# An audio tower on one core: head 4 looked up densely in every second batch, and two tables streamed through a ring

## The chip, the core and the metric

One core of a Trainium2 chip runs the whole program. The metric is the device time in microseconds of one execution.
## What is computed

For each of 32 batches: a tokenizer (four strided convolutions with a channel norm, an MLP that gives every time step a weight, and a pooling from 128 steps to 64 channels by the running sum of the weights), a recurrent mixer (a delta-rule attention over 128 rows of 64), and a feed-forward layer of eight heads with product keys. The last one is what the change touches:

```python
q = (x @ Wq_pk).reshape(b, n, P, HEADS, DIM_KEY).transpose(2, 0, 1, 3, 4)
sim = jnp.einsum('pbnhd,pkhd->pbnhk', q, pk_keys)              # 2 x 64 key scores of each row and head
scores, idx = jax.lax.top_k(sim, PK_TOPK)                      # the best 16 of either side
...
final_scores, pk_idx = jax.lax.top_k(score, FINAL_TOPK)        # the best 16 of the 256 sums
final_scores = jax.nn.softmax(final_scores, axis=-1)
...
k = jnp.einsum('bnhk,bnhkd->bnhd', kv_scores, keys_table[ind])   # 4096 rows of 64 for each head
v = jnp.einsum('bnhk,bnhkd->bnhd', kv_scores, values_table[ind])
```

k and v of a head then take part in a causal attention over the 128 rows. So each row needs, for each head, the weighted sum of 16 rows out of a table of 4096 rows of 128 numbers (key and value side by side).

## The kernel before

The weighted sum is made in two ways. Heads 0 to 4 (NG = 5) are **gathered**: DVE works out the 16 row numbers, POOL fetches 128 table rows with one indirect DMA (L1090), 16 of them a head and so 80 a batch, into one of three buffers `got`, and PE adds them up with 16 weighted matmuls (L1381; the trace shows 32 records) and a transpose (L1387). Heads 5 to 7 (`DENSE`, ND = 3) are **dense**: the whole table of the head lies in SBUF (`tab`, 16 KB in each partition for each head, loaded once), and a head goes through it in 16 units of 256 table rows. A unit is: PE makes the sums of both key scores and a rank distance for 256 x 128 pairs (`pair_scores`, L1337 and L1339, four bf16 matmuls into one of two banks), ACT takes the exponential (L1642), DVE sets those outside the chosen 16 to zero (L2203), and PE multiplies by the table (`table_sum`, L1359). ACT copies the head's sum out after its last unit (L1651). Before its units a dense head needs a distance of each key from the chosen ones (DVE, L2150 and L2155, twelve instructions a head), transposes (L1317, L1318), a split into three bf16 parts, and a trip of these parts through DRAM (`parts`) to the layout `stacked`, by 12 DMAs a head that SP issues.

All engines work on several batches at a time. Each stage of a batch (tokenizer, mixer, `route` for heads 0 to 3, `second` for heads 4 to 7, dense, sums of gathered heads, heads) is cut into hops. The tables `AT` (and `OWN` for the first three and last three batches) give each hop a position in a batch's time; batch b stands b * STEP later. `plan()` sorts all hops by position, and every engine's queue is written in that one order. A hop's position is no time on the chip: it only sets what stands before what in each queue. The order has the dense units of one batch follow on those of the batch before: the units run without a break over the whole program, with pieces of the other stages of other batches between them.

POOL holds nothing but the gathers. Before each head it waits for the row numbers (`s_rows`, `s_single`), and at each fourth gather for the buffer to be read (`s_summed`).

Of the kernel before, what the change touches and what calls it, by code (L numbers as in the profile page):

```python
# [20 lines left out]
ALU = mybir.AluOpType  # L21
ACT = mybir.ActivationFunctionType
# [17 lines left out]
DENSE = (5, 6, 7)  # L40
ND = len(DENSE)
NG = HEADS - ND
# [3 lines left out]
UNITS = ND * TILES  # L46
# [16 lines left out]
QUARTER = 4  # L63
PARTS = 4
# [74 lines left out]
def tower(nc, x, consts, pairs, w0, w1, w2, w3, cvec, mw1, mw2, mw3, mb1, mb2, mb3, stack, mix, bw, ba, bg, vec64,  # L139
          wo_attn, gn, wqpk, keys, wq, table, wo_ffn, parts, out):  # L140
    ctx = ExitStack()
    with ctx:
# [135 lines left out]
        tab = sb("tab", [P, ND, CHUNKS, P])  # L278
# [83 lines left out]
        s_stack = [sem(f"s_stack{i}") for i in range(2)]  # L362
        s_pairs = sem("s_pairs")
# [33 lines left out]
        block = ctx.enter_context(nc.Block())  # L397

# [31 lines left out]
        for n, k in enumerate(("xd", "proj", "lora", "ss", "tri", "p0", "t0", "p1", "t1", "p2", "t2", "p3", "t3", "p4", "t4",  # L430
# [8 lines left out]
        R2 = {k: n for n, k in enumerate(each_list + [  # L439
            "idx", "cand", "keys", "fin8", "codes", "code", "rep_f0", "rep_f1", "rep_f2", "rep_f3", "fin16_0", "fin16_1", "fin16_2", "fin16_3", "fidx",  # L440
            "place", "early", "shift", "pick_e0", "row_e0", "pick_l0", "row_l0",
            "row_d", "row_t", "rep_d", "row_h", "code0", "chosen", "code1", "depth", "code2", "code3"]
            + [f"{k}{i}{j}" for i in range(ND) for j in range(2) for k in ("miss", "near", "half", "dist")]
            + ["fsum", "frec", "weight", "w_t", "shifted"], 1)}
        NROUTE, NSECOND = len(R), len(R2)
# [20 lines left out]
        def group_hops(u):  # L466

            last = u == UNITS - 1
            return ([(f"v{u - 1}", 0.9)] if u else []) + ([(f"k{u - 1}", 0.4)] if u and u % TILES == 0 else []) + (
                [(f"p{u + 1}", 1.2)] if not last else []) + ([("s2", 0.1)] if u == TILES else []) + (  # L470
                [(f"x{u}", 0.6), (f"w{u}", 0.8)]) + ([(f"v{u}", 0.9), (f"k{u}", 0.4)] if last else [])
# [12 lines left out]
        def choose_hops(pieces):  # L484
            return ([("r0", 1.2), ("r1", 1.2), ("r2", 2.2), ("r3", 1.2), ("r4", 1.2), ("cands", 0.5), ("keys", 0.5), ("fin8", 0.8), ("codes", 1.2),
                     ("finx", 0.7), ("repf", 1.0), ("fin16", 0.8), ("fidx", 0.7), ("early", 0.5), ("shift", 0.4), ("e", 0.0)]
                    + [x for k in range(pieces) for x in ((f"e{k}", 1.0), (f"l{k}", 1.2), (f"lr{k}", 1.1))])
# [1795 lines left out]
```

## Time and profile before

| | us |
|---|---|
| median of 3 runs | 3446.4 (3445.68 to 3448.38) |
| span of the profiled execution | 3442.5 |
| PE busy / weight loads | 3091.9 (90%) / 2384.2 (69%) |
| DVE busy | 2856.3 (83%) |
| ACT busy | 2103.0 (61%) |
| POOL busy | 2469.3 (72%) |
| DMA engines, mean busy share | 0.27 at 71 GB/s |

Busy time of an engine is the time in which at least one of its instructions was running. An instruction's time holds its latency, and the next one may start before it ends, so a busy share near 90% is not yet a full engine. POOL's gap between two indirect DMAs is listed as "issue": it waits for nothing there. The profiled span lies 3.9 us under the median of the runs.

### The profile page before, as it was taken

The page shows a single profiled execution, that of the slowest core. Times are in us where ns is not written, and L with a number is a line of the kernel's source. Part 1 is how long each engine was busy: PE and PEld are TensorE (multiplying, and loading weights), DVE is VectorE, ACT ScalarE, POOL GpSimd, SP SyncE. Part 2 cuts the span into 40 slices and gives each one's busy share as a digit, 9 for nine tenths or more (in the row PEclk, how much of TensorE's full clock was granted, in tenths as well). Part 3 has the DMA queues.
Part 4 walks back from the last instruction along what each step waited for, and adds up shares of the span by engine and source line. Part 5 has one row for each costly group of instructions (what it writes and reads, how often), then busy time and mean ns, then how long its engine had stood idle before and what let it go on. Part 6 is the DMA issues. An engine that isn't in the chain of part 4 may idle for free.

```text
span 3442.5 us, 79362 instructions
## 1 busy us (share of the span) xinstructions
PE 3091.9 (90%) x25850; PEld 2384.2 (69%) x25850; DVE 2856.3 (83%) x14978; ACT 2103.0 (61%) x5921; POOL 2469.3 (72%) x2571
## 2 busy tenths in 40 slices
PE   9999999889999989999999999998999999888777
PEld 6776667677667666666767766776766676766666
DVE  3688888988888988888898888888888888888762
ACT  5456666666666666666566666666666666665333
POOL 0177777777777777777777777777777777777774
PEclk9999999999999999999999999999999999999888
DMA  7022222222222222222222222222222222222221
GB/s 159 11 74 71 72 66 69 74 74 76 69 74 61 74 75 75 74 69 69 65 75 73 75 68 75 61 74 74 74 75 69 71 64 75 75 75 68 66 77 41
DMA packets 307373, 245.84 MB, mean 71 GB/s; under 512 B 246600, under 2 KB 259440, under 8 KB 306832
## 3 DMA queue, kind: packets, MB, share of 16 engines
q0 software_dynamic: 81920, 167.94, 17.8%
q1 hardware_dynamic: 225040, 72.83, 9.1%
q8 instruction: 206, 3.38, 0.4%
q14 instruction: 207, 1.70, 0.2%
HBM read 230.06 MB, written 10.49 MB: 70 GB/s over the span
## 4 chain that ended last, share of the span: by engine, by line
POOL 53%; issue 19%; PE 16%; DVE 9%; ACT 4%; DMA 0%; POOLq 0%; SPq 0%; DVEq 0%; ACTq 0%
POOL got L1090 53%; PE bank L1359 3%; PE bank L1180 3%; DVE d_w L2203 1%; PE bank L1198 1%; PE bank L1109 1%; PE bank L1337 1%; PE bank L1339 1%; PE bank L1381 1%; DVE top L1938 1%; PE bank L1126 1%; DVE dist L2155 0%; DVE topi L1942 0%; DVE pick L2150 0%; ACT L1432 0%
## 5 line engine op out<-in xcount | busy, mean ns | idle before, releaser
L1090 POOL DMA_INDIRECT got<-in_table,rows x2560 | 2466.4, 963 | 936.9 <-issue 777.7
L1359 PE MATMUL bank<-d_w,tab 128*128 128x128 f32 x6144 | 1055.9, 295 | 136.5 <-DVE d_w L2203 128.9
L1359 PEld LDWEIGHTS bank<-d_w,tab 128*128 128x128 f32 x6144 | 827.4, 195 | 325.3 <-DVE d_w L2203 214.5
L2203 DVE SCALAR_TENSOR_TENSOR d_w<-bank,d_w 128x256 f32<-128x256 f32 x1536 | 633.6, 414 | 168.3 <-ACT d_w L1642 159.0
L1642 ACT ACTIVATE d_w<-bank 128x256 f32<-128x256 f32 x1536 | 579.6, 380 | 276.6 <-PE bank L1339 258.5
L1337 PE MATMUL bank<-stacked,stack_sel 128*128 128x128 bf16 x3072 | 428.5, 222 | 12.3 <-issue 11.5
L1339 PE MATMUL bank<-d_dist,sel 128*128 128x128 bf16 x3072 | 428.7, 222 | 0.0
L1180 PE MATMUL bank<-h,conv_w 128*128 128x512 f32 (+2 forms) x1024 | 330.6, 469 | 0.5 <-DVE h L1789 0.4
L1337 PEld LDWEIGHTS bank<-stacked,stack_sel 128*128 128x128 bf16 x3072 | 306.8, 100 | 35.0 <-issue 15.2
L2155 DVE TENSOR_REDUCE dist<-pick 128x32 f32<-128x512 f16 x384 | 261.7, 682 | 6.6
L1180 PEld LDWEIGHTS bank<-h,conv_w 128*128 128x128 f32 x1024 | 171.8, 189 | 119.7 <-issue 109.2
L1339 PEld LDWEIGHTS bank<-d_dist,sel 128*128 128x128 bf16 x3072 | 240.7, 99 | 0.0
L1381 PE MATMUL bank<-got,spread_w 128*32 128x128 f32 x5120 | 176.6, 277 | 52.6 <-DMA got<-in_table,rows 28.5
L1518 ACT ACTIVATE square<-bank,cbias 128x512 f32<-128x512 f32 (+2 forms) x96 | 48.7, 508 | 250.2 <-PE bank L1180 250.1
L1381 PEld LDWEIGHTS bank<-got,spread_w 128*32 128x32 f32 x5120 | 135.6, 110 | 90.9 <-issue 79.3
L2150 DVE TENSOR_TENSOR pick<-misses,key_codes 128x256 f16<-128x256 f16 x768 | 190.3, 282 | 0.0
L1432 ACT ACT_TABLE_LOAD x128 | 164.2, 1283 | 3.0 <-PEq L2251 0.7
L1163 PE MATMUL bank<-shared 64*128 64x512 f32 x248 | 138.3, 637 | 7.4 <-DVE normed L1749 7.2
L1198 PE MATMUL bank<-mlp,normed 128*128 128x512 f32 x256 | 118.4, 605 | 24.6 <-ACT normed L1462 24.6
L1167 PE MATMUL bank<-square,cst 128*128 128x512 f32 x248 | 133.8, 621 | 7.2 <-ACT square L1442 7.2
L1451 ACT ACTIVATE h<-normed,chan 128x512 f32<-128x512 f32 x124 | 100.4, 810 | 61.1 <-DVE normed L1770 61.1
L1683 ACT ACTIVATE prob_t<-bank 128x128 f32<-128x128 f32 x256 | 70.8, 277 | 95.9 <-PE bank L1419 95.5
(329 smaller groups left out, 6391.6 us busy)
## 6 DMA issues: line engine op xcount, KB each, us to landing
got<-in_table,rows POOLq DMA_INDIRECT x2560, 2.5
stacked<-parts SPq DMA_DIRECT2D x576, 64.0 KB
parts<-d_parts SPq DMA_DIRECT2D x32, 288.0 KB
stacked<-parts SPq DMA_DIRECT2D x576, 16.0 KB
tab<-in_table SPq DMA_DIRECT2D x24, 256.0 KB, 8.3
got<-in_pairs SPq DMA_DIRECT2D x1, 2048.0 KB, 9.7
shared<-in_x SPq DMA_DIRECT2D x32, 50.0 KB
mlp<-in_mw SPq DMA_DIRECT2D x1, 1024.0 KB, 8.9
```

What stands on the lines that cost most here:

```text
L1090: pool.indirect_dma_start(got[:, n % NGB, k, :], None, table, bass.IndirectOffsetOnAxis(ap=rows[:, b % 2, g * TOPK + k:g * TOPK + k + 1], ...
L1180: last = mm(conv_bank[:, 0:LEN[n - 1]], conv_w[n][:, k, :], rhs, start=k == 0, stop=k == taps - 1)
L1198: last = mm(conv_bank[:, :], z1[:, k, :], mlp2[:, k, :], start=k == 0, stop=k == MC - 1)
L1337: mm(ps[:, x * P:(x + 1) * P], stack_sel[:, x, :], stacked[:, n % 2, tile, :], start=x == 0, stop=False)
L1339: last = mm(ps[:, (2 + x) * P:(3 + x) * P], sel[:, c + x, :], d_dist[:, b % 2, i, :], start=False, stop=x == 1)
L1359: last = mm(acc_bank[:, i * P:(i + 1) * P], tab[:, i, 2 * tile + x, :], d_w[:, u % 2, x, :], start=tile == x == 0, stop=tile == TILES - 1 ...
L1381: last = mm(kv_rows_ps[t * BLOCK:(t + 1) * BLOCK, :], spread_w[:, at:at + BLOCK], got[:, n % NGB, k, :], start=i == 0, stop=i == QUARTER - 1)
L1432: exp_and_ln = lambda: nc.scalar.preload_act_table_set("natural_log_exp_and_others")
L1642: a(d_w[:, u % 2, :, :].rearrange("p k t -> p (k t)"), pair_bank[u % 2][:, 0:2 * P], ACT.Exp).then_inc(s_d_exp, 1)
L2150: return tt(apart[:, a:a + quarter_keys, :], misses[:, upper, i, k, :].unsqueeze(1).broadcast_to(full), key_codes[:, a - upper * half:a - ...
L2155: return v.tensor_reduce(dist[:, i, k, at:at + half], apart[:, at:at + half, :], AX.X, ALU.min, apply_absolute_value=True)
L2203: stt(both, pair_bank[u % 2][:, 2 * P:4 * P], TOPK - 0.5, both, ALU.is_lt, ALU.mult).then_inc(s_d_w, 1)
```

## The change

- `KIND` gives each batch a kind, N and E in turn. An N batch is as before: heads 5 to 7 dense, 0 to 4 gathered. In an E batch head 4 is dense too: 64 units in place of 48, and 64 gathers in place of 80. For the E batches all of DVE's work that finds row numbers and weights for a fifth gathered head is left out (`if ng`, `if single(b)`), and head 4 takes the dense steps: its distances, its transposes, its share in the bf16 parts and its 12 DMAs.
- Only the tables of heads 6 and 7 stay in SBUF. Those of heads 4 and 5 lie in DRAM in quarters (`stream`, 128 partitions x 4 KB = 512 KB) and go through a ring of three quarters. A quarter serves four units. When its last unit has been multiplied, SP, which waits for that, issues the load of the quarter three further on; PE waits for a quarter to have landed before its first unit. An N batch streams 4 quarters and an E batch 8, together 192. SBUF for tables goes from 48 to 44 KB in each partition.
- The positions are one table for each kind, and all are new. Of `OWN` only the tokenizer and the mixer of batch 0 are left: first and last batches otherwise go by the tables of their kind. The number of hops goes from 16224 to 17248. Batch 31 is of kind E.
- Counters that were b * 48, b * 5 and so on are running sums over the kinds.

The core of the diff (the position tables, about 490 lines, and the renamed counters are left out):

```diff
-DENSE = (5, 6, 7)
-ND = len(DENSE)
-NG = HEADS - ND
+KIND = "NENENENENENENENENENENENENENENENE"
+FOUR = "E"
+ND, NG = 4, 5
+RESIDENT = 2
...
+RING = 3
...
-        tab = sb("tab", [P, ND, CHUNKS, P])
+        tab = sb("tab", [P, RESIDENT, CHUNKS, P])
+        ring = sb("ring", [P, RING, CHUNKS // QUARTER, P])
...
+        def nd_of(b):
+            return 4 if KIND[b] in FOUR else 3
...
+        def streamed(b):
+            return nd_of(b) - RESIDENT
+
+        G0, D0, S0_, Q0 = before(ng_of), before(nd_of), before(single), before(lambda b: streamed(b) * QUARTER)
...
+        def after_sum(b, u):
+            refill = u // TILES < streamed(b) and u % QUARTER == QUARTER - 1
+            return ([(f"t{u // QUARTER}", 0.1)] if refill else []) + ([(f"k{u}", 0.4)] if u % TILES == TILES - 1 else [])
...
+            def refill(n):
+                b = max(x for x in range(BATCH) if Q0[x] <= n)
+                h, q = ng_of(b) + (n - Q0[b]) // QUARTER, n % QUARTER
+                sp.dma_start(ring[:, n % RING, :, :].rearrange("p c d -> p (c d)"), stream[h - HALF, q, :, :]).then_inc(s_ring[n % RING], 16)
...
+                def spread_parts(i):
...
+                yield from spread_parts(0)
+                yield from spread_parts(1)
+                for u in range(units(b)):
+                    if u and u % TILES == 0 and u // TILES + 1 < nd:
+                        yield from spread_parts(u // TILES + 1)
+                    if u // TILES < streamed(b) and u % QUARTER == QUARTER - 1:
+                        n = Q0[b] + u // QUARTER
+                        if n + RING < Q0[BATCH]:
+                            yield f"t{u // QUARTER}"
+                            if u % TILES == TILES - 1:
+                                sp.wait_ge(s_d_sum, D0[b] + u // TILES + 1)
+                            else:
+                                sp.wait_ge(s_ring_used, n - n // QUARTER + 1)
+                            refill(n + RING)
 
...
+            for n in range(RING):
+                refill(n)
...
-                for g in range(NG):
+                for g in range(ng_of(b)):
...
-                for i, h in enumerate(DENSE):
+                for i, h in enumerate(range(ng_of(b), HEADS)):
...
+                n = Q0[b] + u // QUARTER
+                if i < streamed(b) and u % QUARTER == 0:
+                    pe.wait_ge(s_ring[n % RING], (n // RING + 1) * 16)
                 for x in range(2):
-                    last = mm(acc_bank[:, i * P:(i + 1) * P], tab[:, i, 2 * tile + x, :], d_w[:, u % 2, x, :],
+                    c = 2 * tile + x
+                    of = ring[:, n % RING, c % (CHUNKS // QUARTER), :] if i < streamed(b) else tab[:, i - streamed(b), c, :]
+                    last = mm(acc_bank[:, i * P:(i + 1) * P], of, d_w[:, u % 2, x, :],
                               start=tile == x == 0, stop=tile == TILES - 1 and x == 1)
                 if tile == TILES - 1:
                     last.then_inc(s_d_sum, 1)
+                elif i < streamed(b) and u % QUARTER == QUARTER - 1:
+                    last.then_inc(s_ring_used, 1)
 
             def group(b, g):
...
-                yield "fidx"
-                for h in range(first, gathered):
-                    own(f"fin16_{h - first}")
-                    last = v.max_index(finp[:, h, 8:16], fin[:, h, 8:16], cand[:, h, :])
-                inc(last)
...
+                if ng:
+                    yield "fidx"
+                    for h in range(first, gathered):
+                        own(f"fin16_{h - first}")
+                        last = v.max_index(finp[:, h, 8:16], fin[:, h, 8:16], cand[:, h, :])
+                    inc(last)
...
+
+                if single(b):
+                    yield "row_d"
+                    own("row_l0")
+                    inc(cp(row_d[:, :, :], rowf[:, h:h + 1, :].broadcast_to([P, 2, TOPK])))
...
+    streamed = table[HALF * NKEY * NKEY:(HEADS - RESIDENT) * NKEY * NKEY].reshape(2, 2, 8, 4, 2, BLOCK, P)
...
+        "wq": t["ffn_Wq"], "table": table, "stream": np.transpose(streamed, (0, 4, 1, 3, 5, 2, 6)).reshape(2, QUARTER, P, -1), "wo_ffn": t["ffn_Wo"],
```

## Rows read from the trace of the kernel before

**Rows 1.** Windows of POOL's gathers (L1090): stretch, busy us (count), clock, DMA share, GB/s.

```profile
430.00:3010.00 2580.00, 1959.15 (x2035) 0.99 0.27 71
...
3354.70:3442.50 87.80, 39.62 (x42) 0.85 0.16 43
```

**Rows 2.** Waits of POOL from 430 to 3010: us in all, times, longest.

```profile
POOL got L1090 <- PE bank L1381: 1.7, 3, 0.7
POOL got L1090 <- DVE rows L1930: 0.9, 3, 0.3
```

**Rows 3.** Timeline of POOL: start, duration, the idle before and what ended it.

```profile
1001.54 0.94 POOL L1090 DMA_INDIRECT got<-in_table,rows  x1 [0.30 <-issue]
1002.78 0.94 POOL L1090 DMA_INDIRECT got<-in_table,rows  x1 [0.30 <-issue]
```

**Rows 4.** Windows of all engines: PE, PEld, DVE, ACT, POOL busy (counts), clock, DMA share.

```profile
430.00:3010.00 2580.00, 2349.46 (x19926) 1799.16 (x19925) 2250.99 (x11854) 1662.87 (x4707) 1959.15 (x2035) 0.99 0.27 71
```

**Rows 5.** Timeline of PE: one dense unit and the start of the next.

```profile
1504.96 0.66 PE L1359 MATMUL bank<-d_w,tab 128*128 128x128 f32 x4
1505.46 0.28 PE L1337 MATMUL bank<-stacked,stack_sel 128*128 128x128 bf16 x2
...
1505.68 0.55 PE L1359 MATMUL bank<-d_w,tab 128*128 128x128 f32 x3
```

**Rows 6.** Timeline of DVE near 1001 us.

```profile
1001.78 0.40 DVE L2203 SCALAR_TENSOR_TENSOR d_w<-bank,d_w 128x256 f32<-128x256 f32 x1
1002.10 0.28 DVE L1906 SCALAR_TENSOR_TENSOR og<-og,mrstd 128x64 f32<-128x64 f32 x1
```

**Rows 7.** Windows of DVE's unit instruction (L2203): stretch, busy us (count).

```profile
217.00:3354.70 3137.70, 613.46 (x1488) 0.99 0.27 71
3354.70:3442.50 87.80, 20.15 (x48) 0.85 0.16 43
```

**Rows 8.** Groups of DVE by shape, 430 to 3010: count, busy us, mean ns, idle before.

```profile
L2203 DVE SCALAR_TENSOR_TENSOR d_w<-bank,d_w 128x256 f32<-128x256 f32 x1222 | 503.9, 414 | 85.8 <-ACT d_w L1642 78.5
L2155 DVE TENSOR_REDUCE dist<-pick 128x32 f32<-128x512 f16 x301 | 205.2, 682 | 5.2
L2150 DVE TENSOR_TENSOR pick<-misses,key_codes 128x256 f16<-128x256 f16 x603 | 149.4, 282 | 0.0
L2030 DVE TENSOR_TENSOR pick<-code,place 128x216 f32<-128x216 f32 x260 | 89.0, 374 | 0.0
...
L2039 DVE TENSOR_REDUCE rowf<-pick 128x8 f32<-128x432 f32 x26 | 15.4, 593 | 0.0
...
L2183 DVE STREAM_TRANSPOSE weight_t<-weight 128x32 f32<-128x32 f32 x25 | 5.0, 200 | 0.0
...
L1981 DVE CAST topf<-topi 128x16 f32<-128x16 uint32 x25 | 4.1, 163 | 0.0
```

**Rows 9.** Groups of PE, 430 to 3010.

```profile
L1359 PE MATMUL bank<-d_w,tab 128*128 128x128 f32 x4887 | 830.3, 293 | 87.2 <-DVE d_w L2203 80.8
L1339 PE MATMUL bank<-d_dist,sel 128*128 128x128 bf16 x2444 | 338.1, 220 | 0.0
```

**Rows 10.** Timeline of PE near 1045 us: a gathered head's sum and the next instruction.

```profile
1045.39 1.08 PE L1381 MATMUL bank<-got,spread_w 128*32 128x128 f32 x32
1046.40 0.71 PE L1359 MATMUL bank<-d_w,tab 128*128 128x128 f32 x4
```

**Rows 11.** Waits of DVE, 430 to 3010: us in all, times, longest.

```profile
DVE res L1913 <- PE bank L1298: 52.4, 25, 2.1
DVE top L1938 <- ACT sims L1608: 44.2, 25, 1.8
```

**Rows 12.** DMA issues: KB each, median us to landing.

```profile
tab<-in_table SPq DMA_DIRECT2D x24, 256.0 KB, 8.3
...
conv_w<-in_w SPq DMA_DIRECT2D x1, 512.0 KB, 3.4
```

**Rows 13.** Timeline of PE in the last batch: the longest wait for gathers.

```profile
3388.77 1.94 PE L1381 MATMUL bank<-got,spread_w 128*32 128x128 f32 x32 [11.63 <-DMA got<-in_table,rows]
```

More of the change, by code:

```diff
@@ L397, in tower, with ng_of, single, before @@
         block = ctx.enter_context(nc.Block())
+        def nd_of(b):
+            return 4 if KIND[b] in FOUR else 3
+        def ng_of(b):
+            return HEADS - nd_of(b)
+        def single(b):
+            return ng_of(b) > HALF
+        def before(count):
+            return [sum(count(x) for x in range(b)) for b in range(BATCH + 1)]
+        def streamed(b):
+            return nd_of(b) - RESIDENT
+        G0, D0, S0_, Q0 = before(ng_of), before(nd_of), before(single), before(lambda b: streamed(b) * QUARTER)
+        LAST_SUM = G0[BATCH] - 1
+        def units(b):
+            return nd_of(b) * TILES
+        def last_batch(b, has):
+            return next((x for x in range(b - 1, -1, -1) if has(x)), None)
         def head_at(b, p):
@@ L973, in program @@
             def program(b):
-                for u in range(count):
+                for u in range(count(b)):
                     yield from unit(b, u)
@@ L2117, in second @@
-                inc(removed(2))
+                for i in range(1, nd - 1):
+                    removed(i)
+                inc(removed(nd - 1))
                 yield "row_h"
-                own("row_t")
-                inc(ts(row_h[:, :], row_t[:, HALF, :], const("half", 0, 1), float(h * NKEY * NKEY), ALU.mult, ALU.add))
-                inc(ts(misses[:, 0, :, 0, :], topi[:, ds, 0, :], KEY_STEP, float(TOPK), ALU.mult, ALU.add))
+                if single(b):
+                    own("row_t")
+                    inc(ts(row_h[:, :], row_t[:, HALF, :], const("half", 0, 1), float(h * NKEY * NKEY), ALU.mult, ALU.add))
@@ L2122, in second @@
+                if not single(b):
+                    own("idx")
+                inc(ts(misses[:, 0, 0:nd, 0, :], topi[:, ds, 0, :], KEY_STEP, float(TOPK), ALU.mult, ALU.add))
                 yield "chosen"
                 own("rep_d")
[L2124 removed]
+                inc(ts(chosen[:, 0:nd, :], cand[:, ds, :], LOWEST, None, ALU.is_equal))
                 yield "rows"
[L2126 to L2127 removed]
@@ L2205, in group @@
             def group(b, g):
-                n = b * NG + g
+                n = G0[b] + g
                 yield f"b{g}"
```

320 lines of the change are left out of this document (174 added, 146 removed), and 527 rows, old and new, of tables (AT, OWN).

## The prediction

> **What bounds the kernel now.** The page's busy shares name PE (90%) and DVE (83%), and POOL only with 72%, so I looked first at who waits. Every gather lasts 0.94 us, and 0.30 us after its end the next one starts [rows 3]; that gap is listed as "issue", nothing outside POOL ends it, so a gather costs POOL about 1.25 us. In the steady stretch from 430 to 3010 us, 2035 gathers ran, one every 1.268 us [rows 1], and in all that time POOL waited 1.7 us for a buffer and 0.9 us for row numbers [rows 2]. It is full without a break. The units of DVE show the period of a batch: 1488 of them, 31 batches of 48, in 3137.7 us [rows 7], 101.2 us a batch, and 80 gathers by 1.268 us are 101.4 us. So POOL's gathers set the period, and the other engines' idle time is a consequence: DVE is busy 2250.99 of 2580 us, 88.3 us a batch with 12.9 idle, PE 92.2 us a batch, ACT 65.2 [rows 4].
>
> Before the first unit lie 217 us, and from the last batch's first unit to the end there are 87.8 us [rows 7]. The profiled span is 217 + 31 x 101.2 + 87.8 = 3442, and the median of the runs is 3.9 us more. I predict with time = 308.7 + 31 x P, where P is the mean period of N and E batches and 308.7 = 217 + 87.8 + 3.9.
>
> **POOL, removed.** An E batch has 64 gathers, so the mean is 72 a batch: 101.2 x 72 / 80 = 91.1 us. This is the floor of P, 10.1 us lower than now. The question of the whole change is how much of that the other engines give away.
>
> **DVE, added in an E batch.** Sixteen more unit instructions by 503.9 / 1222 = 0.412 us are 6.6; eight distance steps by 149.4 / 603 = 0.248 are 2.0; four reductions by 0.682 are 2.7 [rows 8]. One more match-replace, one more shift and some wider instructions have no row of their own in this size; between 0.5 and 1.5 us by what such instructions cost in the same view, I take 1.1. Sum 12.4. **Removed:** two misses by 89.0 / 260 = 0.342, 0.7; a reduction, 0.6; and 27 small instructions (casts, sums of codes, index searches, copies, the row numbers' transposes and the weights), of which the cast with 0.163 and the transpose with 0.200 us are typical [rows 8]; by 0.19 they are 5.1. Sum 6.4. Net +6.0 in an E batch, +3.0 in the mean: DVE goes from 88.3 to 91.3 us a batch, as the view counts busy time. That is as much as POOL's floor. But the view counts too much: the unit instruction that starts at 1001.78 lasts 0.40 us, and the next one starts after 0.32 [rows 6]. Where the next instruction doesn't depend on it, some 0.08 us of each lie under it. A full DVE could go a little under 91.3.
>
> **PE, added.** A unit takes 1505.68 - 1504.96 = 0.72 us from start to start [rows 5], so 16 take 11.5; two transposes, by their width about a unit's bf16 pair each at most, 0.3. Removed: a gathered head's sum, 1046.40 - 1045.39 = 1.0 us [rows 10], and its transpose, 0.2. Net +10.6 in an E batch, +5.3 in the mean. How full PE is now can't be read off its 92.2 us of busy time: the two bf16 pairs and the table product list 0.66 + 0.28 + 0.28 us and take 0.72. The Trainium skill, in "Perfetto Trace Analysis", section "Identifying the Most-Contended Engine", says the same of matmul busy time and wants the weight loads' share looked at instead; they are busy for 1799.16 of 2580 us here, 70%, and by that PE has room.
>
> **ACT** gets 16 exponentials and loses two copies, about +6 us in an E batch on an engine with 36 us idle in each: nothing, as long as DVE and PE, who wait for it, are not late by it.
>
> **What takes the place of POOL's limit.** At P = 91.1, DVE would have no idle time left in the view's count. Its order holds two waits that every batch repeats, because nothing ready stands between: 25 times 2.1 us for the attention's output (L1913) and 44.2 us in 25 for the key scores (L1938) [rows 11], together 3.8 us a batch. Today they lie beside POOL's gathers and cost nothing. If they stay and everything else closes, P = 91.3 + 3.8 = 95.1; if they are filled by the new order, P is POOL's 91.1. Of 0.08 us under the next instruction some comes back. I take 94.0, nearer to the upper of these two, since PE's load rises as well and the idle time of today is 12.9 and not 3.8.
>
> **The ring.** The streamed tables add 192 loads of 512 KB, 101 MB, about 31 GB/s to the 71 of today; the DMA engines' share of 0.27 [rows 4] goes to about 0.36 in proportion. A load is issued when its slot's quarter is used up and is needed eight units later. The mean unit at P = 94 is 94 / 56 = 1.68 us, so the cover is 13.4 us; if the units ran as fast as PE can, 8 x 0.72 = 5.8 us. Landing: the load of the same shape (`conv_w`, 512 KB) took 3.4 us, and the `tab` loads, 256 KB in a queue of 24, 8.3 us [rows 12]. So 0 us, and at the worst pair 2.5 us a quarter, six quarters a batch, 15 us. The longest landing and the shortest cover have no reason to meet at each quarter; I take 0, by the load of the same shape. SP gets 192 more issues and 16 x 12 for the fourth head; each new wait on SP stands in front of the later DMAs of `stacked`, the wave load and the output's store. They wait for events that the order has before them, so a delay there is the skew of the queues; 0 taken, and it is part of the 2.5 above if it isn't. PE's new wait for a quarter has all of PE's queue behind it, and with it ACT and DVE.
>
> **Start and end.** The order holds 224 hops before the first row numbers instead of 238, of the same stages, and one table load less to wait for: 217 stays, give or take 8. In the last batch there are 64 units for 48, at today's 87.8 / 48 = 1.83 us another 29 at most; against it stand 16 gathers (20 us) fewer in the batch, whose last ones PE there waits 11.63 us for at a time [rows 13]. Between -12 and +29; I take 0, as the gathers and not the units hold that stretch: 42 of them fall into it, 53 of its 87.8 us [rows 1]. The loss of the special order for the last three batches is in the same bounds.
>
> **Sum:** 308.7 + 31 x 94.0 = 3222.7. Forecast 3223 us, its own range 3160 to 3280 (P of 92 to 96).
>
> **Rivals.**
> A, POOL stays full: P = 91.1 to 92, 3133 to 3160 us. For it: POOL is kept full today to within 3 us in 2580 [rows 2], with PE busy for 91%. Against: DVE then has no idle time at all by the view's count.
> B, DVE and PE hand each other waits: with half of DVE's idle time of today left, P = 91.3 + 6.5 = 97.8, 3341 us; the case reaches from 3280 to 3435. For it: the unit instruction alone waited 85.8 us in this stretch for ACT [rows 8], and PE 87.2 us before its table product [rows 9], in a period that had slack. Against: those waits could stand because POOL was the limit.
> C, slower: DVE's order needs its 12.9 us of idle time whatever POOL does. P = 91.3 + 12.9 = 104.2, 3539 us; it turns from gain to loss where more than 101.2 - 91.3 = 9.9 us a batch stay idle. The Trainium skill, in the section named above, takes the engine with the highest occupancy as the one that bounds; by that rule it would be DVE here (87% of the stretch against POOL's 76%), a kernel that gains nothing by fewer gathers and pays for what DVE gets. Against it: POOL's gaps of 0.30 us count as idle there, and it didn't wait.
> D, PE is as full as its busy time says. The table product is 830.3 / 4887 x 64 = 10.9 us a head and the bf16 pairs 338.1 / 2444 x 64 = 8.9 [rows 9], with 1.4 off for the gathered sum: +18.4 in an E batch, P = 92.2 + 9.2 = 101.4 or more, 3452 us and up. Start to start [rows 5] speaks against it.
> E, the ring is late by its worst case: P = 94 + 15 = 109, 3688 us; the gain is gone at 1.2 us a quarter.
>
> **Chances.** Forecast 0.47, A 0.12, B 0.31, C 0.04, D 0.04 (half of it within 0.2%), E 0.02. About 0.2% (7 us) is what a measurement of this kernel can tell from no change. Faster: 0.47 + 0.12 + 0.31 = 0.90; same 0.02; slower 0.08. For 8 in 10 the range takes the forecast, the most of A and the nearer two thirds of B: 3138 to 3370.
>
> **What would show it.** Right: POOL's gathers still one every 1.25 to 1.31 us in an E and N pair, with some 2 to 5 us a batch of waits for row numbers or buffers; DVE busy for over 95% in the steady stretch; 56 units a batch on the mean in 94 us; no wait of PE for the ring over 0.1 us in the mean; the end of the last batch within 12 us of 88. A shows POOL without waits, B gaps in both DVE and PE with each other's names and POOL waiting over 6 us a batch, C and D one of these two engines at its old idle time, E a wait of L1359's successor for the ring's DMA. What would make it wrong first is the 94.0: each us of it is 31 us of the result.

## The result, and the profile after

The changed kernel is slower by 1.4%: 3495.5 us median of 4 runs (3485.7 to 3504.7), against 3446.0 us (3445.4 to 3448.4) of the kernel before beside it, ratio 1.0141 [1.0116, 1.0166]. Forecast were 3223 us and a range of 3138 to 3370. The profiled execution spans 3499.2 us.

From the page of the changed kernel: its span, the busy time of each engine, and the chain that ended last by engine.

```profile
span 3499.2 us, 82970 instructions
...
PE 3249.0 (93%) x27402; PEld 2591.8 (74%) x27402; DVE 2991.1 (85%) x14994; ACT 2209.7 (63%) x6161; POOL 2225.0 (64%) x2315
...
PE 72%; DVE 14%; ACT 8%; issue 2%; DMA 2%; SPq 1%; POOL 0%; DVEq 0%; POOLq 0%
```

The same line of the page of the kernel before:

```profile
POOL 53%; issue 19%; PE 16%; DVE 9%; ACT 4%; DMA 0%; POOLq 0%; SPq 0%; DVEq 0%; ACTq 0%
```

POOL has left the chain, as the change meant it to: before, 53% of the chain were gathers and 19% "issue", mostly the gaps between them. PE has come into its place.

Windows of the unit instruction (now L2020) of the changed kernel: stretch, length, busy us (count), clock, DMA share, GB/s. They answer [rows 7]; the last two are one N and one E batch.

```profile
231.50:3422.35 3190.85, 708.12 (x1728) 0.97 0.38 98
3422.35:3499.20 76.85, 26.84 (x64) 0.97 0.29 73
645.10:741.80 96.70, 19.64 (x48) 1.00 0.36 91
741.80:846.80 105.00, 26.26 (x64) 1.00 0.44 111
```

3190.85 / 31 = 102.9 us is P, forecast 94.0. The pair of batches shown last ran wholly at the full clock; it took 201.7 us, 100.9 a batch. Against the kernel before the span grew by 3499.2 - 3442.5 = 56.7 us: 14 at the start (231.5 for 217.4), 3190.85 - 3137.7 = 53 in the 31 periods, and 11 less at the end (76.85 for 87.8).

All engines of the changed kernel from 430 to 3010 us (against [rows 4]):

```profile
430.00:3010.00 2580.00, 2429.29 (x20695) 1930.65 (x20694) 2318.53 (x11682) 1712.73 (x4801) 1734.04 (x1798) 0.97 0.38 98
```

A batch here is 102.9 us, so PE is busy 96.9 us a batch (92.2 before), DVE 92.5 (88.3) with 10.4 idle (12.9), ACT 68.3 (65.2).

What POOL waited for in that stretch: us in all, times, longest (against [rows 2]); and two of its gathers (against [rows 3]).

```profile
POOL got L881 <- DVE rows L1732: 278.8, 25, 14.2
POOL got L881 <- PE bank L1179: 35.3, 17, 3.5
```

```profile
1000.95 0.94 POOL L881 DMA_INDIRECT got<-in_table,rows  x1 [0.30 <-issue]
1002.20 0.94 POOL L881 DMA_INDIRECT got<-in_table,rows  x1 [0.30 <-issue]
```

A gather costs what it cost, 1.25 us, and POOL stands still for 314.1 us in 25 batches, 12.5 each. The gathers that were taken away did free POOL. The batch didn't get shorter by it.

### The profile page after: what moved, and what is told of

Read it like the earlier page. It is cut to its first block, busy times and chain, and to the rows that moved or that the text cites. A ratio compares the mean times of both kernels' runs of the same rounds, so it can differ in the third digit from the quotient of the medians.

```text
span 3499.2 us, 82970 instructions
## 1 busy us (share of the span) xinstructions
PE 3249.0 (93%) x27402; PEld 2591.8 (74%) x27402; DVE 2991.1 (85%) x14994; ACT 2209.7 (63%) x6161; POOL 2225.0 (64%) x2315
## 4 chain that ended last, share of the span: by engine, by line
PE 72%; DVE 14%; ACT 8%; issue 2%; DMA 2%; SPq 1%; POOL 0%; DVEq 0%; POOLq 0%
PE bank L1155 21%; PE bank L971 9%; PE bank L1128 5%; PE bank L1130 4%; PE bank L1179 4%; PE bank L954 3%; DVE d_w L2020 3%; PE bank L958 3%; PE bank L1214 2%; DVE topi L1744 2%; ACT d_w L1442 2%; PE bank L900 2%; PE bank L989 2%; PE bank L917 2%; PE bank L1054 1%
## 5 line engine op out<-in xcount | busy, mean ns | idle before, releaser
L881 POOL DMA_INDIRECT got<-in_table,rows x2304 | 2222.0, 964 | 1226.5 <-issue 686.7
L2020 DVE SCALAR_TENSOR_TENSOR d_w<-bank,d_w 128x256 f32<-128x256 f32 x1792 | 735.0, 419 | 196.1 <-ACT d_w L1442 175.8
L1442 ACT ACTIVATE d_w<-bank 128x256 f32<-128x256 f32 x1792 | 665.4, 381 | 323.9 <-PE bank L1130 296.4
L1155 PE MATMUL bank<-d_w,tab 128*128 128x128 f32 x4096 | 683.5, 291 | 67.8 <-DVE d_w L2020 65.3
L1155 PEld LDWEIGHTS bank<-d_w,tab 128*128 128x128 f32 x4096 | 556.7, 196 | 143.1 <-DVE d_w L2020 112.9
L1155 PE MATMUL bank<-d_w,ring 128*128 128x128 f32 x3072 | 544.9, 302 | 65.4 <-DVE d_w L2020 64.5
L1128 PE MATMUL bank<-stacked,stack_sel 128*128 128x128 bf16 x3584 | 503.3, 223 | 35.4 <-issue 34.9
L1155 PEld LDWEIGHTS bank<-d_w,ring 128*128 128x128 f32 x3072 | 427.6, 201 | 145.4 <-DVE d_w L2020 124.4
L1130 PE MATMUL bank<-d_dist,sel 128*128 128x128 bf16 x3584 | 503.1, 223 | 0.0
L1128 PEld LDWEIGHTS bank<-stacked,stack_sel 128*128 128x128 bf16 x3584 | 359.2, 102 | 83.9 <-issue 60.7
L1130 PEld LDWEIGHTS bank<-d_dist,sel 128*128 128x128 bf16 x3584 | 284.2, 100 | 0.0
```

Source lines behind the costliest of these rows:

```text
L881: pool.indirect_dma_start(got[:, n % NGB, k, :], None, table, bass.IndirectOffsetOnAxis(ap=rows[:, b % 2, g * TOPK + k:g * TOPK + k + 1], ...
L1128: mm(ps[:, x * P:(x + 1) * P], stack_sel[:, x, :], stacked[:, n % 2, tile, :], start=x == 0, stop=False)
L1130: last = mm(ps[:, (2 + x) * P:(3 + x) * P], sel[:, c + x, :], d_dist[:, b % 2, i, :], start=False, stop=x == 1)
L1155: last = mm(acc_bank[:, i * P:(i + 1) * P], of, d_w[:, u % 2, x, :], start=tile == x == 0, stop=tile == TILES - 1 and x == 1)
L1442: a(d_w[:, u % 2, :, :].rearrange("p k t -> p (k t)"), pair_bank[u % 2][:, 0:2 * P], ACT.Exp).then_inc(s_d_exp, 1)
L2020: stt(both, pair_bank[u % 2][:, 2 * P:4 * P], TOPK - 0.5, both, ALU.is_lt, ALU.mult).then_inc(s_d_w, 1)
```

## Experiments

Each time stands beside runs of the kernel before on the same chip (3441.9 to 3445.6 us). P is (first unit of the last batch - first unit) / 31, read from the unit instructions of each trace as above; "end" is from that last batch's first unit to the end of the span. These three are of the profiled execution, which took up to 10 us more than the median of its runs (e8 10, e9 9, the changed kernel 6): a P can stand 0.3 us too high by that.

```
                                      us   ratio to before          P   start  end
before                            3446.0                        101.2   217.4  87.7
changed kernel                    3495.5   1.0141 [.0116,.0166] 102.9   231.5  76.8
e1_noring                         3496.3   1.0163 [.0134,.0193] 102.8   231.5  76.7
e2_ring_old_split                 3446.7   1.0022 [.0008,.0037] 101.3   217.9  87.1
e3_old_order                      4069.5   1.1830 [.1795,.1864] 121.3   218.6  89.6
e4_half_gathers                   3467.3   1.0065 [.0043,.0088] 101.9   230.5  76.7
e5_load_on_before                 3551.1   1.0304 [.0287,.0321] 104.7   218.4  89.1
e6_pe_light                       3351.3   0.9734 [.9715,.9752]  98.2   231.6  74.1
e7_dve_light                      3441.1   0.9983 [.9966,.9999] 101.2   227.5  77.1
e8_both_light                     3298.4   0.9578 [.9556,.9600]  96.8   228.8  76.0
e9_before_72_gathers              3422.5   0.9937 [.9920,.9953] 101.1   217.6  78.2
e10_before_half_gathers           3408.7   0.9899 [.9882,.9915] 100.7   216.9  67.9
e11_pe_load_on_before             3506.1   1.0180 [.0163,.0197] 103.1   217.9  89.4
e12_dve_load_on_before            3479.0   1.0099 [.0082,.0116] 102.3   218.8  87.6
e13_filled_waits                  3445.1   1.0013 [.9998,.0027] 101.2   230.5  76.8
e14_load_half_gathers             3532.4   1.0265 [.0248,.0282] 104.4   218.3  72.6
e15_more_filled                   3436.0   0.9982 [.9973,.9992] 100.9   229.0  77.0
e16_filled_before                 3427.4   0.9962 [.9948,.9976] 100.7   217.4  84.6
```

### The ring, the order, the gathers

The theory at this point was that PE and DVE together can't do the mean batch in less than some 102 us; the rivals were the ring and the order.

e1 has no refills and no waits for them, and the streamed heads read a resident table:

```diff
-                    pe.wait_ge(s_ring[n % RING], (n // RING + 1) * 16)
-                    of = ring[:, n % RING, c % (CHUNKS // QUARTER), :] if i < streamed(b) else tab[:, i - streamed(b), c, :]
+                    of = tab[:, i % 2 if i < streamed(b) else i - streamed(b), c, :]
```

> The changed kernel (3495 us) without the ring's loads and waits: the streamed heads multiply by the resident tables of heads 6 and 7 instead (so heads 4 and 5 get wrong table rows), and no quarter is loaded. All queues of PE, ACT, DVE and POOL keep their order and their other work. Theory 'ring' (its 100 MB of loads delay the stacked parts and the gathers, or PE waits for quarters): 3400 us or less, at least 3 us a batch. Theory 'full engines' (PE and DVE can't do a mean E and N batch in less than some 102 us in any order) and theory 'order' (the engines have room, the new order of the hops makes them wait for each other): 3475 to 3500, under 20 us of gain.

3496.3 us, the changed kernel's time. The ring, its 101 MB of loads and the waits for them cost nothing that shows.

e2 has every batch as N, with the ring and with the hop positions of the kernel before:

```diff
-KIND = "NENENENENENENENENENENENENENENENE"
+KIND = "NNNNNNNNNNNNNNNNNNNNNNNNNNNNNNNN"
```

> The changed kernel with all 32 batches of kind N (3 dense heads, 5 gathered), in the hop order of the kernel before, its own tables for the first and last three batches included; the refills stand right behind the table product that frees their quarter. It differs from the kernel before only by the ring: 128 loads of 512 KB and the waits on them. Theory 'ring': above 3480 us. Theories 'order' and 'full engines': 3440 to 3460, since POOL stays the limit.

3446.7 us, 0.2% more than before, with an interval of 0.1 to 0.4%. With the old split the ring costs some 5 us, if anything.

In e3 both kinds get the hop positions of the kernel before; those of the dense hops are stretched over the fourth head in an E batch. The first row of each table:

```diff
-                    -167817, -129581, -123403, -98385, -88268, -69733, 16352, 40119, 79160, 85948, 97692,
...
+                (-150469, -126999, -125820, -85999, -85521, -29163, -16733, 9167, 107578, 137177, 158128, 171437,
...
```

> The change's work and split (N and E in turn, the ring), but the hop order of the kernel before: N batches by its tables, E batches by the same positions with the 64 units spread over the span of the 48, the 16 distance steps over that of the 12, and the fifth gathered head's hops left out. Nothing in it was fitted to the new load. Theory 'order': under 3400 us. Theory 'full engines': 3480 us or more, and more likely above the changed kernel, since its own order is fitted to the load. Theory 'ring' has no claim here beyond 3460 or more.

4069.5 us, P 121.3. An order made for 48 units and stretched loses 18 us a batch with the same work. A part of it is the clock: the mean granted clock is 0.943 here and 0.966 in the changed kernel, which is 226 us more at the lower level, worth some 2 us a batch by what e13 below gave back (an estimate). So the order of the queues is worth far more than any single cost of the sum, and the changed kernel's own order is a good one by comparison. It doesn't tell yet whether a better one exists.

e4 is the changed kernel with every second gather left out:

```diff
                     for k in range(TOPK):
+                        if k % 2:
+                            continue
```

> The changed kernel with every second gather left out (8 of 16 rows a head; the sums read each fetched row twice, so the gathered heads are wrong). POOL has half its work, all else stays. If POOL or the landing of the gathers has any part in the new period: 3440 us or less. If the limit has gone to PE and DVE, as POOL's waits for row numbers in the changed kernel say: 3470 to 3500.

3467.3 us, 28 less, between the two ranges. The gathers cost the changed kernel 1.0 us a batch, but not through their rows: from 430 to 3010 us PE waited for no gathered row, in the changed kernel or here. What shrank is PE's wait ahead of a batch's first unit. It was 26.4 us in the changed kernel (L1128, below, under "The clock"), and here, where the line is L1130:

```profile
PE bank L1130 <- issue: 11.0, 19, 1.5
```

That is 0.6 us a batch less, and 32 us fewer at the lower clock come with it. As shown below, this wait is for the parts' way through DRAM, so the traffic of the gathers beside it is the likely cost; no run tests that alone.

### Load added to the kernel before

e5 has both parts of this edit, e11 the first alone, e12 the second alone:

```diff
-                for x in range(2):
+                for x in (0, 1) if u % 2 else (0, 1, 1):
                     last = mm(acc_bank[:, i * P:(i + 1) * P], tab[:, i, 2 * tile + x, :], d_w[:, u % 2, x, :],
...
+                    if u % 3 == 0:
+                        vec.tensor_reduce(extra[:, 0:1], pair_bank[u % 2][:, 2 * P:3 * P], AX.X, ALU.add)
                     stt(both, pair_bank[u % 2][:, 2 * P:4 * P], ...
```

> The kernel before, with the mean load of the change put on its engines and nothing else changed: PE repeats one table product in every second dense unit (24 a batch, about 5.3 us), DVE a small reduction in every third unit (16 a batch, about 3 us). The repeated product enters the dense sum, so that is counted wrongly. POOL keeps all its gathers, 101.2 us a batch. Theory 'full engines' (DVE and PE can't do the mean load of the change in less than about 102.8 us a batch, whatever the order): the period rises to that of the changed kernel, 3480 to 3550 us. Theory 'order' (the engines have room for that load, the order of the changed kernel makes them wait): POOL stays the limit, 3442 to 3465 us, and POOL's gathers still come one every 1.27 us.

3551.1 us, 105 over before, 1 us above the range of "full engines" and far from the other. The load costs 3.5 us a batch in a kernel whose POOL was thought to cover it. By the view's busy time it is PE's load of the change (96.8 us a batch for 96.9) and somewhat less than DVE's (90.9 for 92.5).

> Only PE's part of the added load: 24 table products more in a batch (5.3 us), on the kernel before; the products are added twice, so the dense sum is counted wrongly. If PE is full at the present period, the whole of the 3.4 us a batch that both loads cost is here: 3530 to 3555 us. If PE has room and DVE doesn't, 3442 to 3470.

> Only DVE's part of the added load: 16 small reductions more in a batch (3 to 4.5 us), on the kernel before. If PE is the full one, next to nothing: 3442 to 3465 us. If the unit's round of ACT, DVE and PE is what costs, a good part of the 3.4 us a batch: 3480 to 3520 us.

PE's part alone costs 62.6 us, DVE's alone 35.4; together 98, near to the 105 of both at once. I had expected PE to carry the whole or nothing, and 3506.1 lies between the two ranges; DVE's 3479.0 is 1 us under the range of the round between ACT, DVE and PE. Each costs, and they nearly add up: neither engine is the bound by itself. The way runs back and forth between them.

### Load taken from the changed kernel

e6 has the first part of this edit, e7 the second, e8 both:

```diff
-                for x in range(2):
+                for x in range(1):
...
-                    stt(both, pair_bank[u % 2][:, 2 * P:4 * P], TOPK - 0.5, both, ALU.is_lt, ALU.mult).then_inc(s_d_w, 1)
+                    stt(one, pair_bank[u % 2][:, 2 * P:3 * P], TOPK - 0.5, one, ALU.is_lt, ALU.mult).then_inc(s_d_w, 1)
```

> The changed kernel with one of each unit's two table products left out, so half of each dense head's table is not summed: PE has about 56 x 0.22 = 12 us less a batch, all waits and all other work as before. If PE is the engine that is full, the period falls until DVE or POOL takes over: 92.5 us and up of DVE, so 3190 to 3280 us. If the wait chain between ACT, DVE and PE sets the pace, half of it or less comes back, 3310 to 3420 us. If DVE alone is full, nothing: 3480 to 3500.

> The changed kernel with each unit's mask done for half of its columns, so half of the dense weights go into the sum unmasked: DVE has about 56 x 0.13 = 7.5 us less a batch, PE what it had. If DVE is the engine that is full, 3495 - 31 x 7.5 = 3260 to 3300 us. If PE is full, under 1 us a batch comes back: 3465 to 3500. If both hand each other waits, something like a third to a half: 3380 to 3440.

> Both leavings-out of the two kernels before at once (half of the table products, masks over half the columns). The sum of the work that is left is 85 us a batch of DVE, 85 of PE, 90 to 91 of POOL (72 gathers by 1.25). Theory 'full engines': POOL or 91 us takes over, 3130 to 3180 us. Theory 'order': part of the waits stay, since the hops still stand where they stood: 3230 to 3330 us, and POOL keeps waits for row numbers of some 5 us and more in a batch.

3351.3, 3441.1 and 3298.4 us; each within the range of the waits between the engines, e7 1 us above it. 12.3 us of PE's work in a batch (an estimate, 56 products by 0.22; its busy time falls by 8.0) give 4.7 of the period back, 7 us of DVE's 1.7, both together 6.1; again they nearly add up, and neither gives back even half of its size. In e8 the period of 96.8 us is still above POOL's 72 x 1.25 = 90 and above either engine's busy time, 85 and 88. A part of what is left is the clock: it was at the lower level for some 335 us in e6 and 377 in e8, against 238 in the changed kernel. By what e13 below gave back for each us, e8's would be worth some 4 us a batch (an estimate). The rest, about 3 us above POOL's 90, would be the order's, queues that stand in a fixed order, tuned for other lengths; no run shows that part by itself.

### Gathers taken from the kernel before

This is the experiment that separates the gain from its price: the gathers go, and nothing comes in.

Shown is e9, half of one head's rows of five; e10 takes half of all heads' rows in the same way:

```diff
-                    for k in range(TOPK):
+                    for k in range(0, TOPK, 2 if g == 2 else 1):
...
-                    pe.wait_ge(s_got[n % NGB], (n // NGB + 1) * 16 * TOPK)
+                    pe.wait_ge(s_got[n % NGB], 16 * sum(TOPK // 2 if m % NG == 2 else TOPK for m in range(n % NGB, n + 1, NGB)))
```

> The kernel before with 72 gathers a batch for 80, the mean of the change, and nothing else changed: half the rows of the third gathered head are not fetched (its sum takes each fetched row twice). This is the gain alone, without the work that the change puts on DVE and PE. If POOL alone holds the batch, as the prediction's floor says, the period falls by 8 x 1.268 = 10.1 us: 3135 to 3160 us. If PE is full right behind it (in the changed kernel it gave back 4.6 us a batch for 12.3 taken away, and load of 5.3 us cost 3.4 on the kernel before, both as if PE counts), the period stops at 97 to 100 us: 3320 to 3410 us.

> The kernel before with half of all gathers left out (40 a batch, each fetched row taken twice). POOL then needs 51 us a batch and holds nothing. What is left is the period that DVE, ACT and PE reach in the order of before, with the load of before. If the floor of the prediction was right, this is far below 3135 us. If PE's load and order hold right behind POOL, it stays at 3320 to 3410, the same as with 72 gathers.

3422.5 us: 21 in place of the 313 that the floor allows, and half of those from the end. The range for PE right behind POOL was 3320 to 3410; this is 12 us above it, and e10's 3408.7 at its edge. With half of all gathers gone it is 35. Windows of the unit instruction (L2203) in e10, as in [rows 7], then all engines from 430 to 3010 us, as in [rows 4], and the chain.

```profile
216.80:3337.05 3120.25, 616.43 (x1488) 0.99 0.18 46
3337.05:3405.00 67.95, 20.18 (x48) 0.95 0.10 24
```

```profile
430.00:3010.00 2580.00, 2356.81 (x19998) 1802.16 (x19998) 2261.64 (x11895) 1669.04 (x4719) 984.09 (x1031) 1.00 0.18 46
```

```profile
PE 52%; DVE 30%; ACT 13%; issue 5%; DMA 0%; DVEq 0%; SPq 0%; POOL 0%; ACTq 0%; POOLq 0%
```

3120.25 / 31 = 100.7 us a batch with POOL busy for 38% of the stretch, against 101.2 with POOL full. DVE still has 100.7 - 88.2 = 12.4 us idle in a batch and PE its 8.7. So this idle time was not a consequence of POOL. The kernel before had two limits of nearly the same length: POOL's gathers, and the path through PE, DVE and ACT in their order, 100.7. POOL's own isn't quite 101.2 either: in e16 below, with all 80 gathers, P is 100.7 too, and POOL's one wait from 430 to 3010 us is this:

```profile
POOL got L1092 <- PE bank L1386: 0.3, 1, 0.3
```

A chain of waits names the longer limit alone, and says nothing on how far behind it the other lies.

The trace of before has a hint of it from the other side: what PE waited for from 430 to 3010 us.

```profile
PE bank L1359 <- DVE d_w L2203: 80.8, 112, 1.4
...
PE bank L1381 <- DMA got<-in_table,rows: 11.3, 15, 2.0
```

The gathered rows have one consumer, PE's sum, and it waited for them for 11.3 us in 25.5 batches, 0.44 us each. With the longest wait at the end [rows 13], 0.44 x 31 + 11.6 = 25 us would have been the estimate of the whole gain from gathers; e9 and e10 measured 21 and 35. It would have been the right size, but such a wait is no bound on the gain: PE waited for no gathered row in the changed kernel's stretch, and half of the gathers were worth 1.0 us a batch there (e4), because they cost at another place.

### The clock

The mean granted clock is 0.966 in the changed kernel and 0.984 in the one before. With its two levels, 2.4 and 1.2 GHz, this is 2 x (1 - 0.966) x 3499 = 238 us at the lower one, and 110 before. In the changed kernel 26 stretches at the lower level lie between 430 and 3010 us, about two in each pair of batches, 154 us in all; in the kernel before there are 4 of 27 us in all, and most of its time at the lower level comes after 3200 us. One of the 26, PE's busy time and clock by windows:

```profile
1486.50:1496.70 10.20, 8.66 (x103) 1.00 0.78 153
1496.70:1506.90 10.20, 10.20 (x63) 0.50 0.17 40
1506.90:1510.30 3.40, 3.24 (x22) 0.99 0.00 0
```

and the waits of PE ahead of it, then PE's longest waits of the whole stretch from 430 to 3010 us:

```profile
1494.05 0.43 PE L1033 MATMUL bank<-tanh_w,lora_w 64*64 64x128 f32 x2 [1.04 <-DVE sig_g L1643]
...
1495.89 0.71 PE L1155 MATMUL bank<-d_w,tab 128*128 128x128 f32 x4 [0.40 <-DVE d_w L2020]
```

```profile
PE bank L1155 <- DVE d_w L2020: 82.7, 127, 1.8
PE bank L1128 <- issue: 26.4, 25, 2.2
PE bank L1033 <- DVE sig_g L1643: 13.5, 13, 1.0
PE bank L1185 <- DMA stacked<-parts: 10.4, 10, 1.0
```

The new order repeats idle places of PE that the old one had seldom: ahead of a batch's first scores (L1128) and of the table product behind them (L1155), ahead of L1033 and ahead of L1185. All 26 stretches begin within 3 us of such a spell, and the next 3.4 to 10.2 us ran at half speed; not each spell is followed by one (L1033 waits 13 times, and 10 of these are).

Two of the releasers in these rows need a second look. The longest wait at L1128, with the last of the twelve DMAs of that head's `stacked`:

```profile
1045.16 0.35 SPq L804 DMA_DIRECT2D stacked<-parts  x1
1048.77 0.27 PE L1128 MATMUL bank<-stacked,stack_sel 128*128 128x128 bf16 x2 [2.22 <-issue]
```

The profile names no releaser, but the semaphore's updates in the trace do: in each of the 25 batches L1128 starts 0.09 us after the last of the twelve has landed, while ACT's copy of the transposed distances, which it also needs, has been done for 12 to 17 us. So this is a wait for the parts' way through DRAM. L1185 is the other way round: it starts 0.05 us after the end of ACT's copy (L1458) each time, and waits for ACT.

The Trainium skill has this pattern in "TensorE: Matmul & The Clock Gate", section "HAM oscillation — how this bites in real kernels", for a kernel that waits on DMA for some 3 to 5 us at a time. The trace agrees that the clock falls again and again behind the same idle places; here they are 0.4 to 2.2 us long, and only L1128's is a wait on DMA.

e13 puts products ahead of these waits; they add zero to the head that is being summed, or write where the next instruction writes anew:

```diff
+            def idle(count):
+                for _ in range(count if open_head else 0):
+                    i = open_head[0]
+                    mm(acc_bank[:, i * P:(i + 1) * P], const("ident", rows=D), qt[0:D, 1, :], start=False, stop=False)
...
                 filled(b, "lora")
+                idle(4 if b and b % 2 == 0 else 0)
...
+                for _ in range(3 if b else 0):
+                    mm(pair_bank[0][:, 0:P], const("ident"), const("ones"), start=True, stop=True)
                 pe.wait_ge(s_d_mask, b + 1)
                 pair_scores(b, 0)
```

> The changed kernel, whole, with products that change no result put ahead of PE's waits after which the granted clock fell in the trace (some 0.9 us of them at each: ahead of the first unit's scores and its table product at the start of a batch, ahead of L1033 in one batch of two, ahead of the first gathered head's transpose in an E batch). PE stands idle there anyway for 0.4 to 2.2 us, so the products themselves should cost nearly nothing. Theory 'clock': the waits cost a second time because the clock is at 1.2 GHz for 3.4 to 10.2 us after each (6.0 us a batch, which cost some 3 us): the time falls by up to 31 x 3 = 90 us, to 3400 to 3440, and the stretches at the lower level go from 43 to under 20. Rival: PE's clock in these stretches holds up nothing, since others are waited for: 3485 to 3510 us.

3445.1 us: 50 us came back, by products that compute nothing. The mean clock is 0.988, which is 83 us at the lower level in place of 238, so each us less of it gave about a third of a us. The stretches at that level went from 43 in the whole run to 17. P fell from 102.9 to 101.2. The expectation had 90 us as the most and 3400 to 3440 as the range; it came out just above that range. (The filler ahead of L1185 was not in place in this run: no head is open there. e15 has it.)

> The kernel before, in its order, with half of the gathers left out and with the mean load of the change on PE and DVE (24 repeated table products and 16 small reductions a batch). Beside the changed kernel with half of its gathers (3467 us) it tells what the new order is worth with POOL out of the way. If loads and gathers add up as single runs did (3409 + 105): 3505 to 3520 us, and the new order is worth some 45 us. If the 105 us of the loads came from POOL being held up: 3440 to 3470, and the new order is worth nothing.

3532.4 us, against 3467.3 of the changed kernel with half of its gathers. With POOL out of the way in both and about the same load (PE busy 96.6 and 96.3 us a batch, DVE 90.7 and 92.3), the new order is worth 65 us, even with the clock that it costs: 2.5 us a batch in P, less 16 us that its later start and longer end take. My 3505 to 3520 was too low: the load costs 124 us here, 105 with all gathers.

e15 adds fillers by unit to e13, e16 does the same on the kernel before:

```diff
+WAITS = {("N", 18): 1, ("N", 42): 5, ("N", 44): 1, ("N", 46): 2, ("E", 4): 1, ("E", 26): 3, ("E", 28): 2, ...
...
+                if tile:
+                    idle(WAITS.get((b, u), WAITS.get((KIND[b], u), 0) if b < 29 else 0))
                 pe.wait_ge(s_d_w, D0[b] * TILES + u + 1)
```

> The changed kernel with fillers ahead of more of PE's repeated waits: those of the units 18, 42, 44 and 46 of an N batch and 4, 26, 28 of an E batch, the transpose at the start of an E batch (where the run before had put none), the long waits of the last three batches, and five places before the first unit. 86 us at the lower clock are left to take. Theory 'clock': half of that time at most comes back, 3400 to 3435 us, under both kernels. Rival: the fillers now stand in the way of as much as they save, 3440 to 3465 us.

> The kernel before with the same kind of fillers ahead of the repeated waits for the unit's weights (43, 45 and five smaller in a batch, and the long ones of the last three batches). Its clock was at the lower level for 113 us, 80 of them after 3200 us, where half of it may come back: 3400 to 3435 us by the theory 'clock'. If the end of the kernel isn't held by PE, or the fillers come in the way: 3438 to 3460 us. In either case the changed kernel is the better one only if its filled version is under this one.

3436.0 us (3429.3 to 3439.8) and 3427.4 us (3426.2 to 3431.4). The changed kernel with its clock kept up is 0.2% better than the kernel before, and the kernel before with the same care is 0.4% better than it was. The lowest time of this study is the filled kernel with the old split. Its lead of 8.5 us is small, and the intervals of the two ratios meet, so the lead is likely and not shown. That the change has no advantage is shown, with a mean clock of 0.996 for it and 0.991 for the other.

The expectations had 3400 to 3435 for both. e16 is inside and e15 1 us above: its mean clock is 0.996, so the clock has nothing more to give, and P stands at 100.9.

## Why the prediction was wrong

**What bounds.** The step that failed is the sentence that POOL's gathers set the period "and the other engines' idle time is a consequence". That POOL was full is right, by [rows 1 to 3] and by e2. The consequence is not: e10 takes half of the gathers away, and DVE's 12.9 us of idle time become 12.4. The floor of 91.1 for P was POOL's own; the next limit, 100.7, was put at 91.3 to 95.1, from DVE's busy time and two of its waits. Even with the clock kept up (e15) P is 100.9, so 6.9 of the 8.9 us by which P was missed lie here.

**DVE and PE, added.** Forecast were +3.0 and +5.3 us a batch. The windows show 92.5 - 88.3 = +4.2 of DVE and 96.9 - 92.2 = +4.7 of PE (with some of the half clock in the latter). The sizes were about right. Their price was not: by the sum they cost nothing but what lifts DVE's total over POOL's 91.1. On the kernel before loads of this size cost 2.0 us a batch on PE (62.6 / 31) and 1.1 on DVE (35.4 / 31), though both engines had idle time.

**94.0.** It took DVE's sum and added the two largest waits of [rows 11]. Those are two of many. A batch of P = 100.7 with 88.2 us of DVE's work and 92 of PE's holds waits at each hand-over between them, and PE's 80.8 us for the unit's weights, which were at hand in [rows 9], were put into rival B alone, as waits that could stand only because POOL was the limit. e10 takes POOL away, and this wait is 84.7 us.

**What the 102.9 is made of.** The runs give steps, each on a kernel of its own, and not a sum: 100.7 is the old order's period without POOL (e10), and the load put on it brings 104.4 (e14). The new order is at 100.9 when the clock is kept up (e15), and the clock that falls in it costs 102.9 - 100.9 = 2.0, of which e13's few fillers gave 1.8.

**The ring.** 0 was right: e1 and the changed kernel are equal within their runs. Rival E fell. The DMA share "in proportion" was a slip: 0.27 x 102 / 71 is 0.39 and not 0.36; measured 0.38.

**Start and end.** "217 stays, give or take 8" was wrong, 231.5: fewer hops ahead of the first row numbers in number, but 14 us more. e3, with the same work in the old positions, starts at 218.6, so the new positions make it; which of them, I didn't look into. The end shortened by 11, inside the bounds of -12 to +29 of which I took 0.

**ACT.** +3 in the mean, measured 68.3 - 65.2 = 3.1.

**The rivals.** C and D, with a chance of 0.04 each, came nearest in number, 1.3 us above and 1.5 under in P. C has DVE's idle time stay whatever POOL does and turns from gain to loss at 9.9 us idle; measured were 10.4. What it has wrong is the owner: it isn't DVE's order alone, since PE's load costs nearly twice what DVE's does (e11, e12) and gives back more (e6, e7). D had PE as full as its busy time, 101.4 and up, and 3495.5 lies in what it left open; but it adds 9.2 us a batch to PE where 4.7 were measured, and in e6 12.3 us less work gave 4.7, so D's number came near by luck. B named the mechanism, each handing waits to the other, and its sign, POOL waiting for over 6 us a batch, is the one that was seen; it was priced at half of the idle time, and of 12.9 us 10.4 stayed. "Start to start speaks against it" was right on the unit's length, 0.72 us, and said nothing on whether PE could use what it had left. The rule of the Trainium skill on occupancy, cited with C, named DVE over POOL by 87% and 76%; as a warning that another engine than POOL holds the batch it was right, and PE, with 91% busy, stands in it by its weight loads, 70%, and by how near it comes to its peak, not by its busy time. The prediction took that 70% as room on PE. The runs don't bear that reading out: the load on PE alone cost 62.6 us (e11), more than that on DVE.

The marks set out ahead: gathers at 1.25 us, right; POOL waits of 2 to 5 us a batch, measured 12.5; DVE over 95% busy, measured 90; PE's wait for the ring none, right.

## What to carry to other kernels

A full engine is a limit; that it is the only one must be shown. A first hint is how long the consumer waited for what that engine makes: here 0.44 us a batch, where 10.1 were counted on. It is a hint and no bound (e4). The cheap and sure test is to take the work away alone, or to add the load alone, before the change is built: e10 is a few lines. Where several queues run in a fixed order and have been fitted to the same period, idle time on them is a part of the path and no free reserve. At the sizes tried here, work added or taken away moved the period by a quarter to two fifths of its own length, and by up to six tenths of the busy time that it adds or takes. And a new order has to be looked at for the idle places that it repeats: here they cost 50 us through the clock alone.

## What the runs showed of the hardware

A PE that is busy for 94% of a stretch can still lose its clock in it. Idle spells of 1 to 2 us were followed by 3.4 to 10.2 us at half speed, about twice in some 200 us; some 240 us of the run in all, against some 110 before, and 50 us of the time came back through fillers. It isn't the amount of idle time: in the kernel before PE was idle for 9% of the steady stretch and not 6, with 54 spells of 0.9 us or more against 63, and the clock fell 4 times there against 26. What makes one place harmful and another not stays open. The streamed quarters (98 GB/s against 71, DMA share 0.38 against 0.27) cost nothing that shows in the changed kernel (e1) and 0.1 to 0.4% of the time with the old split (e2).
